# Cross-attention on one core: batch 1's context turned earlier, the context's sum folded to one product

## The reference

```python
g_x     = conv1x1(g_w, g_b, x_2).transpose(0, 2, 1)
theta_x = conv1x1(theta_w, theta_b, x).transpose(0, 2, 1)
phi_x   = conv1x1(phi_w, phi_b, x_2)
W  = einsum('bnc,bcm->bnm', theta_x, phi_x) / phi_x.shape[-1]
y  = einsum('bnm,bmc->bnc', W, g_x).transpose(0, 2, 1)
wy = conv1x1(w_w, w_b, y)
wy = bn_gamma * (wy - bn_mean) * rsqrt(bn_var + EPS) + bn_beta
return wy + x
```

## Time and profile before

| what | value |
|---|---|
| median of 3 runs | 773.92 us (773.45 to 774.79) |
| the profiled execution | 773.47 us, its span 771.7 us |
| PE | 760.5 us busy, 99% of the span |
| DVE, ACT, POOL | 606.0, 323.5 and 526.3 us busy |
| mean granted TensorE clock | 0.996 of full |
| the chain that ended last | PE 96%, DMA 2%, DVE 1% of the span |
| transfers | 103.19 MB, the queue of the large ones busy 45% of the span |

### The profile page before, as it was taken

The page is one execution under the profiler, slowest core; times in us unless marked ns, Lnnn a source line. Parts: engine busy times, 40 slices in busy tenths (PEclk is TensorE's granted clock), DMA queues, the critical chain, the costliest instruction groups (busy, mean ns, idle before and its releaser), DMA issues.

```text
span 771.7 us, 11939 instructions
## 1 busy us (share of the span) xinstructions
PE 760.5 (99%) x3916; PEld 654.4 (85%) x3916; DVE 606.0 (79%) x1266; ACT 323.5 (42%) x634; POOL 526.3 (68%) x358
## 2 busy tenths in 40 slices
PE   8999799999999999999999999999999999999998
PEld 6687788889888898888889888888888889888886
DVE  3874987968789696887969789696887969788565
ACT  4533442435434353452436444353552436444231
POOL 5939595884949679494885949679494985949500
PEclk9999899999999999999999999999999999999999
DMA  9815538082551817337082651807346082640202
GB/s 276 202 76 114 213 63 265 1 218 110 111 216 32 246 48 190 136 77 249 0 221 105 135 191 37 259 30 190 136 88 238 1 228 97 152 175 1 110 1 109
DMA packets 55417, 103.19 MB, mean 134 GB/s; under 512 B 2506, under 2 KB 38244, under 8 KB 55396
## 3 DMA queue, kind: packets, MB, share of 16 engines
q1 hardware_dynamic: 53264, 101.86, 45.2%
q10 hardware_dynamic: 2132, 1.05, 0.6%
HBM read 69.35 MB, written 33.55 MB: 133 GB/s over the span
## 4 chain that ended last, share of the span: by engine, by line
PE 96%; DMA 2%; DVE 1%; POOL 0%; SPq 0%; ACTq 0%; ACT 0%; issue 0%
PE wbank L775 49%; PE gbank L775 44%; DMA ctx_sb<-in_ctx_dram 2%; PE wbank L950 1%; PE wbank L821 1%; DVE ctxT L538 1%; DVE x_sb L765 0%; PE wbank L799 0%; PE wbank L827 0%; POOL ctxT_lo L334 0%; SPq L281 0%; PE wbank L811 0%; ACT ctxT_hi L388 0%; ACTq L399 0%; DVE x_sb L752 0%
## 5 line engine op out<-in xcount | busy, mean ns | idle before, releaser
L334 POOL TENSOR_TENSOR ctxT_lo<-ctxT,ctxT_hi 128x512 fp32r<-128x512 f32 x124 | 175.6, 1417 | 194.8 <-ACT ctxT_hi L388 194.8
L345 POOL TENSOR_TENSOR ctx_sum<-ctx_sum,ctxT 128x512 f32<-128x512 f32 x108 | 146.7, 1358 | 0.2
L462 ACT ACTIVATE mt<-stage 32x224 fp32r<-32x224 f32 (+1 forms) x180 | 60.2, 334 | 206.0 <-DVE stage L584 202.4
L363 POOL TENSOR_TENSOR x_lo<-x_sb,x_hi 128x1024 fp32r<-128x1024 f32 x60 | 142.0, 2398 | 0.0
L765 DVE SCALAR_TENSOR_TENSOR x_sb<-wbank,const,x_sb 128x512 f32<-128x512 f32 x110 | 77.5, 747 | 69.4 <-PE wbank L775 69.2
L388 ACT ACTIVATE ctxT_hi<-ctxT 128x512 fp32r<-128x512 f32 x124 | 76.2, 626 | 105.5 <-DVE ctxT L538 105.2
L538 DVE STREAM_TRANSPOSE ctxT<-ctx_sb 128x512 f32<-128x512 f32 x124 | 78.6, 681 | 10.2 <-DMA ctx_sb<-in_ctx_dram 10.1
L775 PE MATMUL gbank<-ctxT_lo,ctxT_hi 128*128 128x512 f32 x360 | 84.3, 389 | 0.1
L257 DVE CAST mt<-stage 32x224 fp32r<-32x224 f32 (+1 forms) x300 | 76.9, 256 | 9.5
L775 PE MATMUL gbank<-z_hi,mt 128*128 128x512 f32 x256 | 81.4, 389 | 0.0
L775 PE MATMUL wbank<-x_hi,wt_hi 128*128 128x512 f32 x256 | 81.0, 397 | 0.0
(11 more groups left out here) (124 smaller groups left out, 1482.4 us busy)
## 6 DMA issues: line engine op xcount, KB each, us to landing
x_sb<-in_x_dram SPq DMA_DIRECT2D x16, 2048.0 KB, 7.8
out_dram<-x_sb SPq DMA_DIRECT2D x63, 512.0 KB, 3.1
ctx_sb<-in_ctx_dram SPq DMA_DIRECT2D x60, 512.0 KB, 8.5
ctx_sb<-in_ctx_dram SPq DMA_DIRECT2D x4, 256.0 KB, 5.9
ctx_sb<-in_ctx_dram ACTq DMA_DIRECT2D x4, 256.0 KB, 7.1
x_sb<-in_L_xattn_w_w_dram SPq DMA_DIRECT2D x1, 512.0 KB, 9.0
stage<-in_L_xattn_theta_w_dram SPq DMA_DIRECT2D x1, 512.0 KB, 14.5
phi_nat<-in_L_xattn_phi_w_dram SPq DMA_DIRECT2D x1, 512.0 KB, 13.8
```

Source lines behind the costliest of these rows:

```text
L334: nc.gpsimd.tensor_tensor(ctxT_lo[:, c, :], turned_ctx(b, c), f(ctxT_hi[:, c, :]), ALU.subtract).then_inc(sem_, 1)
L345: nc.gpsimd.tensor_tensor(ctx_sum[:, :], ctx_sum[:, :], src, ALU.add).then_inc(ctxT_used, 1)
L363: nc.gpsimd.tensor_tensor(x_lo[:, k, :], x_sb[par][:, k, :], f(x_hi[:, k, :]), ALU.subtract).then_inc(x_lo_made, 1)
L462: return nc.scalar.activation(dst, src, ACT.Copy)
```

## The change

Three parts. (1) In batch 0, DVE turns chunks 0 to 3 of batch 1's context ahead of theta's low parts, chunks 4 and 5 where 0 to 3 were, and 6 and 7 where 4 and 5 were; ACT's conversions follow. (2) The sum over positions is folded: when `ctx_sum` is complete, ACT copies its rows 64 to 127 into rows 0 to 63 of `fold` (`move_sum`); POOL adds them to rows 0 to 63 as fp32r (`sum_parts`) and as float32 and subtracts one from the other (`fold`); ACT converts that into rows 64 to 127 of `sum_parts` (`pack_sum`). One product with the matrix of ones then replaces two. POOL's part of it comes behind the low parts of `x`, not ahead of them. (3) On PE the column sums move behind `theta(0, (0, 1))`, and in batch 0 behind `t_block(0)`.

```diff
-        sum_hi = sb("sum_hi", [P, C], F32R)
-        sum_lo = sb("sum_lo", [P, C], F32R)
+        fold = sb("fold", [P, C])
+        sum_parts = sb("sum_parts", [P, C], F32R)
...
                     pool.wait_ge(ctxT_used, CH * b + c)
-                    if c == CH - 1:
-                        nc.gpsimd.tensor_tensor(sum_hi[:, :], ctx_sum[:, :], src, ALU.add).then_inc(sum_split, 1)
                     nc.gpsimd.tensor_tensor(ctx_sum[:, :], ctx_sum[:, :], src, ALU.add).then_inc(ctxT_used, 1)
 
             def sum_rest(b):
                 pool.wait_ge(ctxT_used, CH * b + CH)
-                pool.wait_ge(sum_split, 2 * b + 1)
-                nc.gpsimd.tensor_tensor(sum_lo[:, :], ctx_sum[:, :], f(sum_hi[:, :]), ALU.subtract).then_inc(sum_split, 1)
+                pool.wait_ge(sum_moved, b + 1)
+                up = slice(0, P // 2)
+                nc.gpsimd.tensor_tensor(sum_parts[up, :], ctx_sum[up, :], fold[up, :], ALU.add).then_inc(sum_split, 1)
+                nc.gpsimd.tensor_tensor(ctx_sum[up, :], ctx_sum[up, :], fold[up, :], ALU.add).then_inc(sum_split, 1)
+                pool.wait_ge(sum_split, 3 * b + 2)
+                nc.gpsimd.tensor_tensor(fold[up, :], ctx_sum[up, :], f(sum_parts[up, :]),
+                                        ALU.subtract).then_inc(sum_split, 1)
 
             def prep_ctx(b):
-                pool.wait_ge(sum_split, 2 * b)
+                pool.wait_ge(sum_split, 3 * b)
                 for c in range(CH):
                     pool.wait_ge(ctxT_hi_made, CH * b + (c + 1))
                     lo_part(b, c, ctxT_lo_made)
                     sum_up(b, c)
-                sum_rest(b)
...
-            sum_rest(0)
             for k in (2, 3):
                 pool.wait_ge(x_hi_made, k + 1)
                 nc.gpsimd.tensor_tensor(x_lo[:, k, :], x_sb[0][:, k, :], f(x_hi[:, k, :]),
                                         ALU.subtract).then_inc(first_x_lo_pool, 1)
+            sum_rest(0)
 
             def body(b, half, par, nxt, nxt2):
                 if nxt:
                     prep_ctx(b + 1)
                     prep_x(b + 1, 1 - par)
+                    sum_rest(b + 1)
...
+            def move_sum(b):
+                act.wait_ge(ctxT_used, CH * b + CH)
+                nc.scalar.activation(fold[0:P // 2, :], ctx_sum[P // 2:P, :], ACT.Copy).then_inc(sum_moved, 1)
+
+            def pack_sum(b):
+                act.wait_ge(sum_split, 3 * b + 3)
+                hi(sum_parts[P // 2:P, :], fold[0:P // 2, :], sum_packed)
...
             for j in range(1, KC):
                 z_hi_part(j)
+            move_sum(0)
...
                 if not first(b):
                     move_turned()
+                    pack_sum(b)
                     gram_hi_part(0)
...
+                if first(b):
+                    pack_sum(b)
...
                 theta(0)
-                if not first(b):
+                if first(b):
+                    for c in range(RING):
+                        next_hi(c)
+                else:
                     next_hi(4)
                     next_hi(5)
                 for r, m in enumerate(T_ORDER):
                     act.wait_ge(t_taken, KC * b + (r + 1))
                     hi(t_hi[:, m, :], stage[:, r * CI:(r + 1) * CI], t_hi_made)
                 if first(b):
-                    for c in range(RING):
-                        next_hi(c)
+                    next_hi(4)
+                    next_hi(5)
...
                 theta(1)
                 if first(b):
-                    for c in range(RING, CH):
-                        next_hi(c)
+                    next_hi(6)
+                    next_hi(7)
                 if nxt:
                     prep_x(b + 1, half + (1 if par else 0), 1 - par)
+                    move_sum(b + 1)
...
                 if first(b):
                     dve.wait_ge(in_bp, 16)
+                    next_ctx()
                 else:
                     columns_of_s()
                 theta(0)
...
                     chain(nc.vector.tensor_tensor(const[:, :], r3, beta_, ALU.add))
-                    next_ctx()
+                    transpose_chunk(b + 1, 4)
+                    transpose_chunk(b + 1, 5)
...
                 theta(1)
                 if first(b):
-                    transpose_chunk(b + 1, 4)
-                    transpose_chunk(b + 1, 5)
+                    transpose_chunk(b + 1, 6)
+                    transpose_chunk(b + 1, 7)
...
-                    if first(b) and m in (1, 2):
-                        transpose_chunk(b + 1, 5 + m)
...
                 def column_sums():
-                    pe.wait_ge(sum_split, 2 * b + 2)
-                    mm(S_BANK[:, :], ones_r[:, :], sum_hi[:, :], True, False)
-                    mm(S_BANK[:, :], ones_r[:, :], sum_lo[:, :], False, True).then_inc(s_done, 1)
+                    pe.wait_ge(sum_packed, b + 1)
+                    mm(S_BANK[:, :], ones_r[:, :], sum_parts[:, :], True, True).then_inc(s_done, 1)
...
-                else:
-                    pe.wait_ge(work_free, NO * b + (3 - NO))
-                    column_sums()
...
                 theta(0, (0, 1))
                 if first(b):
                     pe.wait_ge(z_taken, 4)
+                else:
+                    pe.wait_ge(work_free, NO * b + (3 - NO))
+                    column_sums()
...
                 theta(0, (2, 3))
-                if first(b):
-                    pe.wait_ge(zb_taken, 1)
-                    column_sums()
                 pe.wait_ge(gram_lo_made, 3 * b + 3)
                 pe.wait_ge(low_lo_made, 2 * b + 1)
                 t_block(0)
+                if first(b):
+                    pe.wait_ge(zb_taken, 1)
+                    column_sums()
                 t_block(1)
```

More of the change, by code:

```diff
@@ L217, in xattn_kernel @@
         ctxT_used = sem("ctxT_used")
-        sum_split = sem("sum_split")
+        sum_moved, sum_split, sum_packed = sem("sum_moved"), sem("sum_split"), sem("sum_packed")
         x_hi_made, x_lo_made = sem("x_hi_made"), sem("x_lo_made")
@@ L952, in body @@
                 theta(0, (2, 3))
+                pe.wait_ge(gram_lo_made, 3 * b + 3)
+                pe.wait_ge(low_lo_made, 2 * b + 1)
+                t_block(0)
                 if first(b):
@@ L955, in body @@
                     column_sums()
-                pe.wait_ge(gram_lo_made, 3 * b + 3)
-                pe.wait_ge(low_lo_made, 2 * b + 1)
-                t_block(0)
                 t_block(1)
```

## The result

The changed kernel takes 767.26 us (median of 6 runs, 766.29 to 767.62) against 773.9 us: a ratio of 0.9909, 95% interval 0.9899 to 0.9919, 6.6 us faster. Forecast were 766.0 us and a range of 763.2 to 769.0. The profiled execution took 767.3 us with a span of 765.3 us, 6.4 less than before.

The account below looks back on a forecast made before the run. PE's own products bound the kernel, besides start-up and a late context load before batch 1. Batch 2 starting 4.6 us earlier plus 3.3 for the product gave 7.9 us off 773.47: 765.6, median 766.0 us, range 763.2 to 769.0.

Parts of the forecast that it names:

- One product, 14 x 0.235 = 3.3 us: In batches 2 to 15, one column-sum product fewer on PE saves 0.235 us each, 3.3 us in all.
- Rival C: Regular batches' DVE chain slips over 0.1 us, so the product's gain goes: 769.3 us, in part 767.5; chance 0.10.
- The fold on POOL and ACT costs nothing in a regular batch: In regular batches ACT's pieces fall into its rests; POOL's three of 1.30 us end 1.3 us before DVE's casts.
- rival E: POOL's sum pieces reach into DVE's casts every batch, costing 14 x 1.2 us: 783 us; chance 0.06.
- Batch 0, chunks earlier: a stall of 0.2 us, 0 to 0.6: In batch 0, transposes ahead of theta's low parts delay a bias addition, stalling PE 0.2 us, bounds 0 and 0.6.
- Batch 0, load earlier: Batch 2's context load issues at 61.4, not 66.11 us; PE's 4.4 us wait in batch 1 shrinks to 0.15.
- Rival D: The context load stays the bound, slower beside outputs: up to 4.6 us given back, 770.6 us; chance 0.03.
- DVE's second step: In batch 1, POOL slows the ten casts by some 2.0 us; last turned row at 82.8 us, PE waits 2.8.
- Rival A: No second wait in batch 1, casts free of POOL: 2.0 us gained, 764.0 us; chance 0.17.
- rival G: Batch 1's casts pay all three POOL sum pieces in full, 3.12 + 3.9 us: 767.9 us; chance 0.06.
- The rest of batch 1, 35.4 us: From batch 1's last Gram row to batch 2's start takes 35.4 us, so batch 2 starts 4.6 us earlier.
- rival B: Clock falls to 1.2 GHz after PE's 2.8 us rest in batch 1: 768.0 to 769.2 us; chance 0.10.

Follow-up runs that it names:

- the longer POOL: Changed kernel with two more POOL operations of 64x512 behind the sum in each batch, into rows nobody reads: 772.36 us, ratio 0.9985.
- the folded sum alone: Changed kernel with batch 0's turning of the context back where it was, keeping the folded sum and moved product: 771.5 us, ratio 0.9968.
- held-back quarter: Changed kernel; in batch 1 alone POOL makes the sum's pieces before x_lo's last quarter, which waits until DVE's casts are done: 765.47 us, ratio 0.9893.
- the filler: Changed kernel with ten further unused 512-column products on PE before the wait for batch 1's last turned row: 766.28 us, ratio 0.99.
- the earlier turning alone: Kernel before the change with only batch 0's turning of the context moved earlier, and ACT's order with it: 770.04 us, ratio 0.9949.
- both series: The changed kernel's first runs and the same kernel run once more beside other runs: medians 767.26 and 767.24 us.
- DVE taking the quarter: Changed kernel; in batch 1 alone DVE, not POOL, makes x_lo's last quarter in its rest before the late context: 765.24 us, ratio 0.9889.

## Why the prediction held, point by point

*One product, 14 x 0.235 = 3.3 us.* Right: 0.227 each, 3.2. The slack behind DVE was put at 0.35 us before the change; the traces now show 0.22 left and, by the longer POOL, 0.29 before PE is really held up. Rival C did not happen.

*The fold on POOL and ACT costs nothing in a regular batch.* Right. Pieces of 64x512 took 1.28 us, as taken, and not half; POOL ended 1.5 us ahead of the casts, where 1.3 was forecast. ACT's pieces took 0.63. The longer POOL shows that rival E's mechanism exists: 0.28 us a batch for 2.2 us more of POOL, which reached 0.7 us into the casts. Its full price of 1.2 was not reached by any run.

*Moving the product costs nothing.* Right, but half the truth: the prediction counted PE's order only, and did not ask for the old place with the new fold. There it costs 0.68 us a batch and turns the change into a loss.

*Batch 0, chunks earlier: a stall of 0.2 us, 0 to 0.6.* It was 0. gram_lo was freed sooner, as argued, and PE began batch 1 at 68.82, not at 68.94; with the folded sum alone, and so without the earlier chunks, it was no sooner there (68.68, in a trace whose chain stood 0.14 us earlier from 26 us on).

*Batch 0, load earlier.* Issue 61.29 (61.4 forecast), DVE 73.59 (73.4), PE's rows 76.53 (76.35), the wait 0.29 (0.15). Right. Rival D did not happen: the load took 12.30 us from issue to DVE, with the outputs behind it.

*DVE's second step.* Casts from 77.30 (77.1), 5.15 us (5.1), the last row at 83.12 (82.8), PE's rest 2.60 (2.8). POOL's x_lo ended at 75.9 (76.0) and its sum at 79.8 (79.9). The held-back quarter shows that the 2 us over 3.12 are POOL's. Rival A (casts free of POOL) and rival G (all three pieces paid, 7.02 us) did not happen. G's 767.9 and the partial C's 767.5 lie nearer to the measured 767.26 than the forecast does, so the number alone would have spoken for the wrong ones; the casts and the period rule them out. For G the casts would have had to start with POOL's first piece; of the three pieces' time they met the last 2.5 us, 77.30 to 79.78.

*The rest of batch 1, 35.4 us.* This is the mis-sized term. Batch 2 begins with its low products:

```profile
119.67 1.52 PE L796 MATMUL gbank<-ctxT_lo,ctxT_hi 128*128 128x512 f32 x6
```

That is 119.67 - 83.12 = 36.55 us. The 1.1 us are the clock, rival B, given 0.10 and priced at 2 to 3.2 us. Among its own signs of being wrong the prediction named a granted clock of 0.5 behind batch 1's rest, and that sign came. By the mean clock, nine of the changed kernel's eleven executions had such a fall: the argument against it, that the rest is shorter than 4.4 us, did not hold, and the chance was far too low. The price was too high: 3.4 us and not 6.8 ran at half speed, which is 1.7 us of PE's work, and a part of that fell on time in which PE would have waited. (With the filler its weight loads stand still for 0.44 us ahead of the Gram transposes, for DVE, and for 0.36 us ahead of `t_block(0)`; in the changed kernel they do neither.) With the clock kept up by filler the kernel takes 766.3, a third of a microsecond from the forecast 766.0.

In sum: 4.6 + 3.3 = 7.9 us were forecast and 6.4 measured in the trace: 0.3 for the later row, 1.1 for the clock, 0.1 for the product. The range held since it had been drawn to take in most of rival B. The forecast itself left B out, and at B's own price it would have been too high.

What stays open: why the clock fell after one rest and not after another of the same length, and where it fell in the two executions with a mean of 0.996 (768.66 us, and 771.56 with the earlier turning alone), which no trace covers.

## What to carry to other kernels

When a wait on the path is removed, follow the engine that was waiting to its next step and look at what runs beside it then; here the load's wait went, and the casts behind it met a GpSimd that was through by the old schedule's time. A saved product is worth its time only if its input is ready at its new or old place: ask for each order of queue, with the new producer, when the input comes. And where TensorE's rest is shortened but not removed, price the clock at either level as a term of the sum with its own chance, not as a rare accident. Look at the granted clock of every execution, too, before a spread is called noise: here it sorts them.

## What the runs showed of the hardware

- The granted clock fell behind a rest of PE of 1.8 us in one execution, of 2.6 us in others and of 4.5 us with the longer POOL, and held through rests of 1.7 and 2.1 us in two more. Before the change it fell in a rest of 4.4 us. No length of rest separates the two in these runs. In the changed kernel, whose traced rests are 2.6 us in both series, two executions of eleven kept a mean clock of 1.0. Ten useless products in the rest made the kernel 1.0 us faster.
- A fall of 3.4 us behind the rest cost 1.1 to 1.2 us: from batch 1's last row to its output stretch it took 30.14 us at full clock (with the filler, and with DVE taking the quarter) and 31.27 and 31.30 us with the fall.
- A cast of DVE that is issued while a GpSimd operation runs waits for its end: 1.26 us behind a piece with 1.1 us to go, 2.07 us in the earlier trace rows. Ten casts beside an idle GpSimd took 3.12 us in the regular batches of every trace but that of the longer POOL. By the Trainium skill, "SBUF — State Buffer", section "Who interferes with whom", a DVE instruction in a two-port mode and one of GpSimd exclude each other, and the one that is issued first keeps the port pair for its whole instruction. The runs agree for the cast that comes second, down to a piece issued 0.01 us ahead of it; no row here shows GpSimd waiting for a cast.
- An operation on 64 partitions by 512 takes as long as one on 128 by 512: 1.28 against 1.30 us on GpSimd, 0.63 against 0.63 on ScalarE.
